# Conditioned ternary feed-forward on one core: the first two token groups by fp32 products of the raw weights, the down products moved further behind

## The reference

```python
def act_quant(x):
    scale = 127.0 / jnp.clip(jnp.max(jnp.abs(x), axis=-1, keepdims=True), 1e-05, None)
    return jnp.clip(jnp.round(x * scale), -128.0, 127.0) / scale

def weight_quant(w):
    scale = 1.0 / jnp.clip(jnp.mean(jnp.abs(w)), 1e-05, None)
    return jnp.clip(jnp.round(w * scale), -1.0, 1.0) / scale
scale = cond @ norm_w.T + 1.0
ms = jnp.mean(x * x, axis=-1, keepdims=True)
h = x * (scale[:, None, :] * jax.lax.rsqrt(ms + EPS))
u = h @ up_w.T
val, gate = jnp.split(u, 2, axis=-1)
h = val * jax.nn.gelu(gate, approximate=False)
y = act_quant(h) @ weight_quant(down_w).T
return y + x
```

## Time and profile before

| | us |
|---|---|
| median of 3 runs | 428.65 |
| lowest, highest | 428.15, 430.88 |
| profiled execution, its own time | 430.21 |
| profiled execution, its span | 428.3 |
| PE busy in it | 407.5 |
| DVE busy in it | 311.7 |

### The profile page before, as it was taken

One profiled execution on the slowest core, in us unless ns is written; L12 is line 12 of the kernel. 1 busy time (PEld: TensorE's weight loads), 2 busy tenths in 40 slices (PEclk: granted clock), 3 DMA queues, 4 the chain that ended last, 5 costly groups with the idle time before them and its releaser, 6 DMA issues.

```text
span 428.3 us, 6396 instructions
## 1 busy us (share of the span) xinstructions
PE 407.5 (95%) x2115; PEld 212.5 (50%) x2115; DVE 311.7 (73%) x625; ACT 172.3 (40%) x393; POOL 117.7 (27%) x169
## 2 busy tenths in 40 slices
PE   6589899999999999999999999999999999999991
PEld 4434445555555545554555555554555455555550
DVE  2858778777877787777877787777877787778761
ACT  2246353534444353534344343434444344433320
POOL 1102132332324132232423232231423242232111
PEclk9969899999999999999999999999999999999996
DMA  7532353736365464837265564837364574534332
GB/s 282 171 108 51 73 71 66 173 75 161 62 176 83 102 132 76 173 73 167 55 171 77 84 149 85 171 66 169 64 136 111 75 160 86 112 73 101 61 100 73
DMA packets 111433, 47.71 MB, mean 111 GB/s; under 512 B 103208, under 2 KB 106920, under 8 KB 111400
## 3 DMA queue, kind: packets, MB, share of 16 engines
q1 hardware_dynamic: 111256, 46.78, 50.8%
q10 hardware_dynamic: 144, 0.52, 0.3%
HBM read 13.60 MB, written 8.52 MB: 52 GB/s over the span
## 4 chain that ended last, share of the span: by engine, by line
PE 93%; DVE 2%; issue 2%; DMA 1%; ACT 1%; POOL 0%; POOLq 0%; SPq 0%; ACTq 0%
PE ps_gate L546 13%; PE ps_gate L544 13%; PE ps_gate L541 13%; PE ps_val L541 13%; PE ps_y L572 13%; PE ps_val L544 13%; PE ps_val L546 13%; DMA norm_sb<-norm_wT 1%; DVE w_lo L404 1%; DVE wmax L388 1%; PE ps_gate L525 1%; PE ps_val L530 0%; DVE top L394 0%; PE ps_y L579 0%; POOL y_out L260 0%
## 5 line engine op out<-in xcount | busy, mean ns | idle before, releaser
L436 DVE SCALAR_TENSOR_TENSOR act_h<-ps_val,comp,gel 128x512 f32<-128x512 f32 x128 | 95.7, 748 | 80.1 <-PE ps_val L546 76.8
L311 ACT ACTIVATE gel<-ps_gate,comp 128x512 f32<-128x512 f32 x128 | 87.5, 686 | 144.1 <-PE ps_gate L546 140.1
L252 POOL TENSOR_TENSOR h_hl<-h,h_hl 128x256 f16<-128x256 f32 x64 | 43.0, 672 | 216.5 <-ACT h_hl L295 216.5
L541 PE MATMUL ps_val<-w_hi,hT 128*128 128x512 f16 x256 | 98.0, 383 | 0.0
L544 PE MATMUL ps_gate<-w_lo,hT 128*128 128x512 f16 x256 | 98.0, 383 | 0.0
L541 PE MATMUL ps_gate<-w_hi,hT 128*128 128x512 f16 x256 | 97.8, 382 | 0.0
L544 PE MATMUL ps_val<-w_lo,hT 128*128 128x512 f16 x256 | 97.7, 382 | 0.0
L442 DVE TENSOR_REDUCE tmax<-act_h 128x1 f32<-128x1024 f32 x64 | 78.1, 1221 | 2.2
L546 PE MATMUL ps_gate<-w_hi,hT 128*128 128x512 f16 x256 | 77.1, 383 | 0.0
L546 PE MATMUL ps_val<-w_hi,hT 128*128 128x512 f16 x256 | 76.1, 379 | 0.0
L572 PE MATMUL ps_y<-dw_q,qT 128*128 128x256 bf16 x512 | 67.2, 275 | 7.5 <-DMA qT<-q_bf 5.3
(11 more groups left out here) (56 smaller groups left out, 211.6 us busy)
## 6 DMA issues: line engine op xcount, KB each, us to landing
x_sb<-x SPq DMA_DIRECT2D x15, 512.0 KB, 4.8
out<-y_out SPq DMA_DIRECT2D x15, 512.0 KB, 3.6
w_in<-up_wT SPq DMA_DIRECT2D x4, 512.0 KB, 6.2
scale_tok<-scale_dram SPq DMA_DIRECT2D x15, 128.0 KB
hT<-h_hl SPq DMA_TRANSPOSE x64, 2.5
dw<-down_wT SPq DMA_DIRECT2D x1, 1024.0 KB, 6.5
qT<-q_bf SPq DMA_TRANSPOSE x64, 3.0
x_sb<-x ACTq DMA_DIRECT2D x1, 512.0 KB, 3.4
```

Of the source, the lines that this page charges most:

```text
L252: nc.gpsimd.tensor_tensor(h_hl[:, g % 2, 1, :], h[:, g % 2, :], h_hl[:, g % 2, 0, :], ALU.subtract)\
L311: nc.scalar.activation(gel[:, u % US, :], ps_gate[u % US][:, :], ACT.Gelu, scale=comp[:, j, GATE:GATE + 1]).then_inc(gelu_ready, 1)
L436: nc.vector.scalar_tensor_tensor(act_h[:, g % 2, j, :], ps_val[u % US][:, :], comp[:, j, VAL:VAL + 1], gel[:, u % US, :], ALU.mult, ALU.mu ...
L541: nc.tensor.matmul(bank[:, :], hs[:, 0, k, :], w_hi[:, j, k, s, :], start=(k == 0), stop=False)
```

## The change

Eight things are changed:

1. The conditioning inputs come in one array and one DMA (`cn_sb`) instead of two. The up weights are laid out by (j, gate or value, k) and loaded one DMA per half, gate before value; the first two groups of x have DMAs of their own on ACT's queue.
2. The scale is also made transposed (`first_scale`: two fp32 products with `norm_sb` as the stationary operand and 8 columns). x of groups 0 and 1 is turned by TensorE (`turn_x`), and DVE multiplies it by that scale while it leaves PSUM (`take_xT`), into `hT32`, fp32.
3. The halves of groups 0 and 1 are two fp32 products each, of `hT32` and the raw fp32 weights (`project_f32`). The token's root mean square goes in afterwards, as the scale of the GELU and of `combine`.
4. The maxima of the weights, their powers of two and both splits move behind these halves on every engine. The powers now go by a diagonal through TensorE: one transpose and one product for the scale and j = 0, one of each for j = 1. The top of the weights' scale is 2^10 instead of 2^14.
5. PE's list at the start is rewritten. Of 46 `keep_awake` transposes 6 are left.
6. `down` for group i stands behind group i + 6 at first, then nearer in four steps, at g = 16, 20, 24 and 28, after which it is i + 2 as before (`downed`). `token_scale` and `quantise` run three groups behind, then two from g = 12, then one from g = 20 (`quantised`). In each group where such a step is made, one more is done.
7. The preparation of the down weights moves from g = 1 and 2 to g = 3 to 5 (ACT), 4 and 5 (DVE), 3 (PE).
8. Buffers: 6 tiles of x instead of 4, 6 `qT` instead of 3, 4 `act_h` instead of 2, 16 `deq` instead of 8.

```diff
-    HS, QS, US = 3, 3, 3
+    F32G = 2
+    XS, HS, QS, US, HA = 6, 3, 6, 3, 4
...
+    def quantised(g):
+        return max(0, min(G, g - (2 if g < 12 else 1 if g < 20 else 0)))
+    def downed(g):
+        behind = 5 if g < 16 else 4 if g < 20 else 3 if g < 24 else 2 if g < 28 else 1
+        return max(0, min(G, g - behind))
...  SP
-            sp.dma_start(cond_sb[:, :], condT).then_inc(cond_loaded, 16)
-            sp.dma_start(norm_sb[:, :], norm_wT).then_inc(cond_loaded, 16)
-            for j in range(NJ):
-                for k in range(KD):
-                    sp.dma_start(w_in[:, j, k, :, :], up_wT[:, j, k, :, :]).then_inc(w_loaded[j][k], 16)
+            sp.dma_start(cn_sb[:, :], cond_norm).then_inc(cond_loaded, 16)
+            load_w(0, GATE)
+            load_w(0, VAL)
+            sp.dma_start(x_sb[:, 0, F32G:NG, :].rearrange("p n d -> p (n d)"), x_tiles[0, :, F32G * D:NG * D])\
+                .then_inc(x_loaded[0], 16)
+            load_w(1, GATE)
+            load_w(1, VAL)
+            load_x(1)
             sp.wait_ge(scale_ready, 1)
             sp.dma_start(scale_dram, scale_nat[:, :]).then_inc(scale_stored, 16)
-            load_x(1)
-            turn_h(0)
-            turn_h(1)
+            turn_h(2)
+            load_scale(1)
+            turn_h(3)
             sp.dma_start(dw[:, :, :], down_wT.rearrange("(f p) d -> p f d", p=P)).then_inc(dw_loaded, 16)
...
-            for g in range(G):
+            for g in range(F32G, G + 1):
...
-                if g >= 1:
-                    turn_q(g - 1)
+                for i in range(quantised(g - 1), quantised(g)):
+                    turn_q(i)
...  ACT
-            high_part(0)
-            high_part(1)
+            gelu(0)
+            gelu(1)
             w_high(0)
+            high_part(2)
+            square(1, 0)
+            square(1, 1)
+            gelu(2)
+            high_part(3)
+            square(1, 2)
+            square(1, 3).then_inc(msq_ready, 1)
             w_high(1)
...  DVE
+            def take_xT(g):
+                dve.wait_ge(xT_turned, g + 1)
+                nc.vector.tensor_tensor(hT32[:, g, :, :].rearrange("p k (b s) -> p (k b) s", s=SP_B),
+                                        ps_xT[:, 0:D].rearrange("p (c s) -> p c s", s=SP_B),
+                                        scaleT[:, :, :].rearrange("p k b -> p (k b)").unsqueeze(2)
+                                        .broadcast_to([P, KD * BT, SP_B]), ALU.mult).then_inc(hT32_ready, 1)
...
+            first_scale()
+            take_xT(0)
+            scale_max()
+            weight_max(0, GATE)
+            weight_max(0, VAL)
+            take_xT(1)
+            scale_first_tile()
+            power_of_two(0, 0, 3)
+            weight_max(1, GATE)
+            take_power(0, 0, 3)
             dve.wait_ge(recip_ready, 1)
             scale_rms(0)
+            weight_max(1, VAL)
+            scale_h(2)
+            weight_comp(0)
+            combine(0)
+            power_of_two(1, 3, 5)
+            scale_h(3)
+            weight_low(0, GATE)
+            take_power(1, 3, 5)
+            weight_low(0, VAL)
+            weight_comp(1)
+            combine(1)
+            dve.wait_ge(recip_ready, 2)
+            weight_low(1, GATE)
+            combine(2)
+            weight_low(1, VAL)
...
-                    token_scale(g - 1)
...
-                    quantise(g - 1)
+                for i in range(quantised(g - 1), quantised(g)):
+                    token_scale(i)
+                    if g >= 4:
+                        dequant_scale(i)
+                    quantise(i)
...  PE
+            def project_f32(bank, g, j, s):
+                for k in range(KD):
+                    ins = nc.tensor.matmul(bank[:, :], hT32[:, g, k, :], w_in[:, j, s, k, :], start=(k == 0),
+                                           stop=(k == KD - 1))
+                return ins
...
-            keep_awake(10)
+            keep_awake(6)
+            pe.wait_ge(cond_loaded, 16)
+            first_scale()
+            turn_x(0)
+            nc.tensor.matmul(ps_nat[:, 0:D], cond_sb, norm_sb, start=True, stop=True).then_inc(nat_summed, 1)
+            half(0, GATE)
+            turn_x(1)
+            pe.wait_ge(rep_ready, 1)
+            pe.wait_ge(scaleT_ready, 1)
+            nc.tensor.matmul(ps_rep[:, 0:D], cond_rep[:, :, :].rearrange("c b s -> c (b s)"), norm_sb,
+                             start=True, stop=True).then_inc(rep_summed, 1)
+            half(0, VAL)
+            pe.wait_ge(scale_ready, 1)
+            rows(0, 0, 3, 3)
+            half(1, GATE)
+            spread(0, 0, 3)
+            half(1, VAL)
+            half(2, GATE)
+            rows(1, 3, 5, 5)
+            pe.wait_ge(scale0_ready, 1)
+            half(2, VAL)
+            spread(1, 3, 5)
+            half(3, GATE)
+            half(3, VAL)
+            for g in range(F32G, G + 2):
...
-                if g >= 2:
-                    down(g - 2)
+                for i in range(downed(g - 1), downed(g)):
+                    down(i)
```

More of the change, by code:

```diff
@@ L12, in cond_bitlinear_ffn @@
     B, S, D = x.shape
-    C = condT.shape[0]
+    C = cond_norm.shape[0]
     FF = down_wT.shape[0]
@@ L69, in cond_bitlinear_ffn @@
         comp = sb("comp", [P, NJ, 2], fp32)
-        w_in = sb("w_in", [P, NJ, KD, 2, CW], fp32)
-        w_hi = sb("w_hi", [P, NJ, KD, 2, CW], fp16)
-        w_lo = sb("w_lo", [P, NJ, KD, 2, CW], fp16)
+        w_in = sb("w_in", [P, NJ, 2, KD, CW], fp32)
+        w_hi = sb("w_hi", [P, NJ, 2, KD, CW], fp16)
+        w_lo = sb("w_lo", [P, NJ, 2, KD, CW], fp16)
         dw = sb("dw", [P, NF, D], fp32)
@@ L92, in cond_bitlinear_ffn @@
         gel = sb("gel", [P, US, CW], fp32)
-        act_h = sb("act_h", [P, 2, NJ, CW], fp32)
+        act_h = sb("act_h", [P, HA, NJ, CW], fp32)
         tmax = sb("tmax", [P, 2], fp32)
@@ L337, in _ @@
                     high_part(g + AHEAD)
-                if g >= 3:
-                    scale_y(g - 3)
-                if g == 1:
+                for i in range(downed(g - 2), downed(g - 1)):
+                    scale_y(i)
+                if g == 3:
                     act.wait_ge(dw_loaded, 16)
@@ L520, in keep_awake, with first_scale @@
                     nc.tensor.transpose(ps_awake[:, 0:P], ident[:, :], ident[:, :])
-            def rows_of(columns):
-                for i, col in enumerate(columns):
-                    ins = nc.tensor.transpose(ps_row[0:1, i * P:(i + 1) * P], col, ident[:, :])
-                ins.then_inc(row_ready, 1)
-            def spread(lo, hi, i):
+            def first_scale():
+                for k in range(KD):
+                    ins = nc.tensor.matmul(ps_scaleT[:, k * BT:(k + 1) * BT], norm_sb[:, k * P:(k + 1) * P],
+                                           cond_sb[:, 0:BT], start=True, stop=True)
+                ins.then_inc(scaleT_summed, 1)
@@ new lines, in turn_x, with rows @@
+            def turn_x(g):
+                pe.wait_ge(x_first[g], 16)
+                if g >= 1:
+                    pe.wait_ge(hT32_ready, g)
+                for k in range(KD):
+                    ins = nc.tensor.transpose(ps_xT[:, k * P:(k + 1) * P], x_sb[:, 0, g, k * P:(k + 1) * P], ident[:, :])
+                ins.then_inc(xT_turned, 1)
+            def rows(i, lo, hi, ready):
+                pe.wait_ge(wmax_ready, ready)
+                if i >= 1:
+                    pe.wait_ge(recip_ready, i)
+                nc.tensor.transpose(ps_chain[0:hi - lo, 0:P], maxima[:, lo:hi], ident[:, :]).then_inc(row_ready, 1)
@@ L529, in spread @@
+            def spread(i, lo, hi):
                 pe.wait_ge(top_ready, i + 1)
-                nc.tensor.matmul(ps_col[:, lo:hi], ones[0:1, :], top_pow[:, lo:hi], start=True, stop=True)\
+                n = hi - lo
+                nc.tensor.matmul(ps_chain[:, P:P + n], ones[0:n, :], top_diag[0:n, i, 0:n], start=True, stop=True)\
                     .then_inc(spread_ready, 1)
-            def weight_rows(j):
-                pe.wait_ge(wmax_ready, KD * (j + 1))
-                rows_of([wmax[:, j, k, s:s + 1] for k in range(KD) for s in (VAL, GATE)])
-                spread(1 + 2 * j, 3 + 2 * j, 1 + j)
@@ L547, in project @@
                                            stop=(k == KD - 1))
                 return ins
-            def unit(u):
+            def project(bank, g, j, s):
+                hs = hT[:, (g - F32G) % HS, :, :, :]
+                for k in range(KD):
+                    nc.tensor.matmul(bank[:, :], hs[:, 0, k, :], w_hi[:, j, s, k, :], start=(k == 0), stop=False)
+                    if g == F32G and k == 0:
+                        pe.wait_ge(wlo_ready, 2 * j + (1 if s == GATE else 2))
+                    nc.tensor.matmul(bank[:, :], hs[:, 0, k, :], w_lo[:, j, s, k, :], start=False, stop=False)
+                for k in range(KD):
+                    ins = nc.tensor.matmul(bank[:, :], hs[:, 1, k, :], w_hi[:, j, s, k, :], start=False,
```

(2 more changed lines are left out.)

369 lines of the change are left out of this document (188 added, 181 removed).

## The result

| | before | after |
|---|---|---|
| median of 4 runs each, us | 429.31 | 414.37 |
| lowest to highest | 428.15 to 430.88 | 413.69 to 414.55 |
| span of the profiled execution | 428.3 | 412.7 |
| its own time | 430.21 | 414.55 |

The ratio is 0.9641, 95% interval 0.9621 to 0.9661: faster by 3.6%. Run again later beside other kernels the changed kernel gave 413.93 and 0.9627 (0.9611 to 0.9643). Forecast was 412.5, which is 0.962 of the median shown then.

The account below looks back on a forecast made before the run. PE bounds the kernel, leaving only the start, one stall and the end. Gains of 12.2 us at the start and 3.9 at the first down product, 16.1 together, off the 428.65 median give 412.5 us; range 408.5 to 418.

Parts of the forecast that it names:

- Start of the first half: Kernel start: PE begins the first fp32 half at 6.8 us, weights just there; bounds 6.3 and 8.0.
- Price of a half: Groups 0 and 1: an fp32 half of two products costs 3.41 us at low clock, 1.72 at full.
- Clock: fp32 stage: full clock comes 5 us behind the first half's start, at 11.8; between 4.0 and 6.8 behind.
- Rival A: Clock stays low through the fp32 stage, leaving 1.6 of 3.9 us gained: 427.0 us; chance 0.06.
- Group 2 starts: End of the fp32 stage: all halves of groups 0 and 1 are through at 24.7 us.
- the yardstick: L597 behind group 1 in the old kernel, two groups projected, at 36.86 us; against it 12.2 us gained.
- Split hidden: Weight split under fp32 halves: DVE ends the fourth `weight_low` at 27.5, PE needs it at 28.8; cost 0.
- Down weights: First down product behind group 6, at 50.7 us: old stall 2.2 and slow stretch 1.7 go, 3.9 gained.
- Rival B: PE waits once or twice more, up to 3.9 us each: 416.4 or 420.3 us; chance 0.14.
- Moved quantisation, double downs: Groups up to g = 28: DVE keeps up, slack 3.5 us at double quantisations, double downs cost 0.
- Rival C: fp32 product of 512 columns costs 2.37 us, loads unhidden and clock low: slower, 437.6 us; chance 0.04.
- Rival D: Quicker start, by earlier clock rise or weights at 6: 2.5 to 3.5 us less, 409.5; chance 0.09.

Follow-up runs that it names:

- e12: Changed kernel with the product of the scale's natural form behind the first fp32 half and 44 identity transposes ahead of the last down product: 414.68 us.
- e11: The changed kernel unaltered, run again later beside other kernels: 413.93 us, ratio 0.9627.
- e8: Changed kernel with 44 identity transposes ahead of the last down product, in PE's wait for the last `qT`: 415.14 us, ratio 0.9662.
- e6: Changed kernel with 10 identity transposes at its start instead of 6: 413.89 us, ratio 0.9640.
- e7: Changed kernel with three more, unused DVE reductions right ahead of the last `w_lo`: 416.18 us, ratio 0.9683.
- e1: Kernel before with its own start, taking only the new lags, larger buffers and later down-weight preparation: 426.44 us, ratio 0.9925.
- e3: Changed kernel with first down product behind group 3 instead of 6, quantisation two groups behind, down weights prepared at g = 2 and 3: 417.94 us.
- e4: Changed kernel with all four catching-up steps made at once, five down products in a row behind group 28: 414.18 us, ratio 0.9653.
- e9: Changed kernel with first gate weights first on SP's queue, conditioning on ACT's, the scale's natural-form product behind the first fp32 half: 417.65 us.

## Why the prediction was right, point by point

- **Start of the first half.** Forecast 6.8, measured 7.14, in the other executions with this front 6.6 to 6.9. It was put on PE's list with the weights "just there", and the two do end close together. In the profiled execution the load came last, 5.7 us from issue against the 5.1 taken from the earlier trace rows; e12 shows that with the small product gone the load alone holds the half until 6.59.
- **Price of a half.** 3.41 and 1.72 forecast, 3.7 at the low clock (with the first load and unhidden parts) and 1.72 measured. The working has each next load of the stationary operand hidden under a record. What it missed is 0.3 in the first half and 0.19 in each of the three that follow `spread` or the repeated scale: 1.91 instead of 1.72. Behind a transposed row (L622, 0.11) a half takes 1.72, so a short instruction ahead doesn't explain it by itself; the reason stays open.
- **Clock.** Forecast 11.8, measured 10.7 in the profiled execution, 9.9 to 15.6 over all with this order of loads: the bounds of 4.0 to 6.8 us behind the start were too narrow on both sides (3.6 in the profiled execution, 3.0 in e11, 8.9 in e8). The rise at 6.8, which the transposes might have brought, was not seen either, even with 10 of them (e6). Rival A did not come about, but its mechanism, products at the low clock, was there for 3.0 to 8.9 us of the stage.
- **Group 2 starts** at 25.17 against 24.7. Too low were the start (0.3), the first half (0.3) and the three loads (0.6 together), too high the rise (about 0.55) and the small instructions. That the sum comes within 0.5 is in part luck, as these cancel. Against the yardstick 11.7 instead of 12.2.
- **Split hidden.** The last `w_lo` was forecast to end at 27.5 and ended at 27.47 (it starts at 26.20 and takes 1.27); slack 1.3 forecast, 1.6 measured by e7.
- **Down weights.** The sum's product at 35.37 (35.1 forecast), `dw_q` at 45.9 (47), the first down product at 51.05 (50.7), no stall. The 3.9 us came: 15.6 - 11.7 in the spans, 3.4 in e1's. Rival B's stalls were absent; e3 shows that they come at once when the lag is cut by three groups, but without the slow stretch that B adds to each.
- **Moved quantisation, double downs:** 0 forecast; no PE wait in the trace, and e4 shows that even five in a row are free.
- **Rival C** fell with the records' 0.43 us each at full clock, and at the low one too: e8's second half, all slow, is 1.83 a product, against C's 2.37. **Rival D** was not seen as a case of its own: the rise came 3 us or more behind the first half, and no median lay under 413.8.

The total was 16.1 against 15.6 in the spans; by the medians 14.9, and 16.2 in the later session.

## What to carry to other kernels

When a bound engine idles at the start for a preparation, look for a dearer form of its work that needs no preparation: the two fp32 groups cost 3.4 us more of PE (at the full clock) than the fp16 ones and bring 11.7, because the split runs under them. Then everything that the first work used to hide must be moved too: the lags here are worth 3 to 4 us and would be missed at once. Price such a move at a point of the bound engine's list which both versions pass, and take the first load's landing, not its issue, as the start.

## What was not expected of the hardware

- The moment at which TensorE's clock rises varied from 9.9 to 15.6 us with the same instructions ahead and PE busy throughout in the last case. It is worth up to 2.5 us of 414 (e8 beside the changed kernel), more than several of the edits. What sets it stays open.
- Waits of 1.2 and 1.5 us in e3 and 1.6 in e7 left the clock at 1.00; one of 2.1 in the kernel before was followed by a fall. Why is open too.
- Identity transposes in fp32 kept the granted clock at 1.00 over 5 us of otherwise idle time (e8, e12).
- A 96 KB load issued in the same microsecond as a 512 KB one on another queue landed at 6.1 us (e9); issued 0.65 us ahead of it, at 4.0.
